# Layernorm variance by eight ScalarE squares with accumulators, and new issue lists

## The chip, the cores and the metric

The kernel runs on one core of a Trainium2 chip (trn2). The metric is the device time in microseconds of one execution. A core has five engines that run side by side, each with its own queue in order: TensorE (PE), VectorE (DVE), ScalarE (ACT), GpSimd (POOL) and SyncE (SP, which here only issues transfers).

## The reference, cut to what matters

A tower of four layers works on 32 sequences of 128 tokens with 64 features. Each layer is `h = h + attention(layernorm(h))` and then `h = h + ffn(layernorm(h))`:

```python
def _layernorm(x, axis=-1, eps=1e-05):
    m = jnp.mean(x, axis=axis, keepdims=True)
    v = jnp.var(x, axis=axis, keepdims=True)
    return (x - m) / jnp.sqrt(v + eps)
```

Layer 0 has attention with decay and a mixture of 16 experts, of which each token uses 2, and one more layernorm inside its ffn; layer 1 has block attention and 32 small experts, one for each token; layer 2 has linear attention with two inner layernorms and a mixture of 8 experts; layer 3 has a linear recurrence along the sequence and a layer with binary (sign) weights. That makes 11 layernorms over the 64 features of every token.

## The kernel before, in words

The 32 sequences are split into 4 units of 8. A unit's activations stand in SBUF as `h` and `xn`, 128 partitions (tokens of a sequence) by 8 sequences by 64 features, that is 128x512. Each unit has its own buffers, two PSUM banks and semaphores, and goes through the whole tower; the four units are independent, and the engines work on them in turn.

For each engine and unit the program is a Python generator (`program(u)`), which issues a few instructions between two `yield`s. Work that belongs to no unit (loading and preparing weights) stands in the generators `setup` and `later`. In which order an engine's queue takes the turns of these generators is written out by hand in `TURNS` (line 44): a string for each engine, where `s` is a turn of `setup`, `t` one of `later` and a digit one of that unit. `in_order` (line 85) plays it. An engine executes its queue strictly in that order, and each instruction waits for its semaphores.

A layernorm is done for a whole unit. DVE sums the features (line 1181) and subtracts the mean (line 1184, into `xn`). ACT squares `xn` with a scale of 1/8 (`square`, line 589, instruction at line 592) into `sq`. `sq` has 65 columns for each sequence: the last one holds epsilon, set once by POOL (line 449). So when DVE sums the 65 columns (line 1190, into `var`, 128x8), it gets variance plus epsilon. POOL raises that to the power -1/2 (`rstd`, line 471, instruction at line 474), DVE multiplies `xn` by it (line 1196, or 1207 for the norms whose result goes into `h`), and PE transposes the result (line 759). There are 11 norms in each of the 4 units, 44 in all. `sq` without its last column also serves as the buffer `y` (line 227), into which POOL gathers the embedding rows (line 441).

In the mixture of layer 0, PE multiplies by an expert's first weights (lines 764 and 765), DVE applies the ReLU as a floor and the gate (line 1286), and PE multiplies by the second weights (line 771). The gates reach all partitions by way of DRAM: SP saves them (line 408) and loads them spread (line 418). Ahead of that stand the routing steps on DVE (`top2`, 20 small steps for a unit). Unit 0's first gated product waits for the last of the prepared matrices of layer 3 (line 1276), unit 1's for the prepared sign weights (line 1279), because their raw data stand in the `hid` buffers of units 0 and 1. In layers 1 and 2, ACT evicts the hidden layer (line 620). In layer 3's last part, PE multiplies by the sign weights (line 1032), ACT evicts the result through Sign (line 711, 64 turns in each unit, 256 in all) and PE sums it up (line 1010). ACT's functions Exp, Gelu and Sin need tables of their own; each change of table is an instruction of its own in the trace (ACT_TABLE_LOAD).

Of the kernel before, what the change touches and what calls it, by code (L numbers as in the profile page):

```python
# [4 lines left out]
P = 128  # L5
D = 64
# [23 lines left out]
BIG = 1.0e30  # L30
LN_EPS = 1e-5
DEN_EPS = 1e-6
GATE_MIN = 2.0 ** -24
# [11 lines left out]
    "SP": (  # L45
        "st000001111100000000101010101010101010101012102222031012012033331202102101203313232121123313232121123332"
        "3222332323232323323232323233330000000010111111112222222323333233330123"
    ),
    "POOL": (
        "sttttttttt0ttttttt1ttttttttttt0tt21323000000111110123122223333203213000000111100211113222232333233223300"  # L50
        "0010110111222333223323"
    ),
    "ACT": (
        "sss00100211100031222011011ttt323322333232300000100110110011021020110302003020123011301322101002112321311"
        "30111233020222203212302312312300313232310231133323220300203130101301201022031133011001121312120223320032"
        "32301230230113203230002023101010103310101100110120100122310101332021021231031023023102123103102302310212"
        "31031230231021023131023023021023131023023120230132132032102130320132132012031032031231201203103203123120"
        "120310320312312012031032031231201231323123121231312323223323232233232322323333"
    ),
    "PE": (  # L60
        "st00001111tt00002221111001102003030030200302220010110103101300103311010011001011010210120130013101200122"
        "10210021212010011230203313233022101021011220303313233221211112230133032033122121032213233122032332233233"
        "32232133120132023013232233221320332320330310030113000002012010213213110321011031021102213111321020132310"
        "22222322322312312313033032033232332123131332320200033001301001010020202111331131011010101202121232320312"
        "30123023023230023001323002310030300100200001011201100011201103001011003112110311000210031101100113110000"
        "12001120110021130021132210022311002231102233110023311002233100223311002231102233110203311002233100223311"
        "00223110223311200331122331002233110022311002233101233110022133002233002231100223311023311002233002233112"
        "23001223300211330221133220033221130022113320013322001133022113322003112200331210033122003311220331122030"
        "11220033121003312200331122033112203011220033121003312200331122033112203011220033121003312203311223311223"
        "011223311233122331122331122311223312331223322332232233233223322332232233233223322332232332333333"  # L70
    ),
    "DVE": (
        "s000sss01t011t1ttt200122t0200ttt0113t03131001200000001000000103t11000111111010101111131t11111t1ttttttttt"
        "tt202t0t202202ttt02tt303202ttt30313031021232012222301302222130313330132320132303332210212323201333331030"
        "10120120120210210120331323021021012033103020302102010012030133203120122310032032001311210003210321311321"
        "30210320301201302300001112312312110001321311032122321321212211323312311113333123302000222032222322222000"
        "23330232333002002031311331230120322202131311333130130130311031010001022201210120100000010101100000012221"
        "32332232231212000001213331231111013313313323221132011001111112032323203020312303232132020321023120321230"
        "23123012302312032302310312031230231203203120333131030011230212101121123030311012312312332223021132332102"
        "32322210332233232133203232323123303223213330213021302130213023120321032103210321032130213213232323"  # L80
    ),
# [47 lines left out]
def tower(nc, ids, emb_w, logs, wa, wb, wc, wd, wup, wrow, binary, ballots, out):  # L129
# [6 lines left out]
    with ExitStack() as ctx:  # L136
# [68 lines left out]
        neg_half = sb("neg_half", [P, SEQS])  # L205
        floor0 = sb("floor0", [P, E0])

        h = per_unit("h", [P, SEQS, D])
        xn = per_unit("xn", [P, SEQS, D])
        sq = per_unit("sq", [P, SEQS, D + 1])  # L210
        total = per_unit("total", [P, SEQS])
# [14 lines left out]

        y = [sq[u][:, :, 0:D] for u in units]
        shifted = [view(fm2[u], 0, W, e=D) for u in units]
# [156 lines left out]
        with nc.Block() as block:  # L385
# [51 lines left out]
            def _(pool):  # L437
# [106 lines left out]
            def _(act):  # L544
# [498 lines left out]
            def _(dve):  # L1043
# [568 lines left out]
```

## Time and profile before

| | |
|---|---|
| three runs | 699.85, 701.21, 702.47 us (median 701.21) |
| the profiled execution, its own time | 703.61 us |
| its span, from the first to the last instruction | 701.8 us |
| mean granted TensorE clock | 0.886 of full speed |
| instructions | 8330 |

The profile is of one execution. Busy time is an engine's time with work on it; PEld is the loading of weights on TensorE, which overlaps the multiplications. In rows by line, `out<-in` are the program's names without the unit's number, then the shapes, the count, the busy time and the mean duration of one, then the engine's idle time before these instructions and what ended it. Two instructions of one engine can overlap, so that the busy time of a group is less than its count times the mean. The chain that ended last is followed back from the last instruction, step by step, to what released it.

### The profile page before, as it was taken

The page shows a single profiled execution, that of the slowest core. Times are in us where ns is not written, and L with a number is a line of the kernel's source. Part 1 is how long each engine was busy: PE and PEld are TensorE (multiplying, and loading weights), DVE is VectorE, ACT ScalarE, POOL GpSimd, SP SyncE. Part 2 cuts the span into 40 slices and gives each one's busy share as a digit, 9 for nine tenths or more (in the row PEclk, how much of TensorE's full clock was granted, in tenths as well). Part 3 has the DMA queues.
Part 4 walks back from the last instruction along what each step waited for, and adds up shares of the span by engine and source line. Part 5 has one row for each costly group of instructions (what it writes and reads, how often), then busy time and mean ns, then how long its engine had stood idle before and what let it go on. Part 6 is the DMA issues. An engine that isn't in the chain of part 4 may idle for free.

```text
span 701.8 us, 8330 instructions
## 1 busy us (share of the span) xinstructions
PE 582.4 (83%) x2951; PEld 319.9 (46%) x2974; DVE 491.8 (70%) x921; ACT 298.4 (43%) x525; POOL 185.6 (26%) x146
## 2 busy tenths in 40 slices
PE   0378669999999999899589677685897999999996
PEld 0166345444335445366454453345543644444442
DVE  0857779966678998967787988878888973333331
ACT  0222231100011122545356445342455379999985
POOL 6783001000031313420527235425216220000000
PEclk9965569999999999998699887765999999999999
DMA  8310234689564530000000013200420000000011
GB/s 212 105 20 1 60 126 134 211 224 337 189 186 154 160 125 32 1 1 2 0 1 0 1 31 124 75 15 6 162 78 1 1 0 1 1 0 1 0 31 30
DMA packets 30777, 49.85 MB, mean 71 GB/s; under 512 B 8400, under 2 KB 8656, under 8 KB 30736
## 3 DMA queue, kind: packets, MB, share of 16 engines
q1 hardware_dynamic: 29136, 46.82, 21.3%
q10 hardware_dynamic: 576, 1.45, 0.9%
q0 software_dynamic: 1024, 1.05, 0.7%
q8 instruction: 23, 0.38, 0.2%
q14 instruction: 18, 0.15, 0.1%
HBM read 47.86 MB, written 1.44 MB: 70 GB/s over the span
## 4 chain that ended last, share of the span: by engine, by line
PE 54%; DVE 26%; POOL 6%; issue 6%; DMA 4%; ACT 3%; SPq 1%; DVEq 0%; another core or an unknown queue 0%
PE ps L771 9%; PE ps L1032 9%; PE ps L1010 7%; PE ps L764 6%; POOL inv_std L474 4%; PE ps L765 4%; DVE hid L1286 2%; DVE total L1181 2%; PE ps L759 2%; POOL sq L441 2%; DVE xn L1196 2%; PE ps L1021 2%; DVE var L1190 2%; PE ps L886 2%; PE ps L823 2%
## 5 line engine op out<-in xcount | busy, mean ns | idle before, releaser
L711 ACT ACTIVATE hid<-ps 128x512 bf16<-128x512 f32 x256 | 134.0, 619 | 30.4 <-PE ps L1032 29.2
L474 POOL TENSOR_TENSOR inv_std<-var,neg_half 128x8 f32<-128x8 f32 x44 | 79.1, 1798 | 192.1 <-DVE var L1190 191.7
L1032 PE MATMUL ps<-xs,w3z 128*128 128x512 f32 x256 | 118.2, 535 | 5.5 <-DVE xs L1488 3.1
L764 PE MATMUL ps<-xs,up_hi 128*128 128x512 f32 x192 | 97.1, 506 | 21.2 <-DVE hid L1286 13.7
L1010 PE MATMUL ps<-hid,kbin 128*128 128x512 bf16 x248 | 96.2, 391 | 1.0 <-ACT hid L711 0.5
L1488 DVE TENSOR_TENSOR xs<-ps,big_a 128x512 fp32r<-128x512 f32 x64 | 43.5, 689 | 75.3 <-PE ps L1021 72.1
L765 PE MATMUL ps<-xs,up_lo 128*128 128x512 f32 x192 | 79.6, 415 | 0.0
L764 PEld LDWEIGHTS ps<-xs,up_hi 128*128 128x128 f32 x192 | 37.8, 197 | 91.3 <-issue 40.8
L771 PE MATMUL ps<-hid,kb 128*64 128x512 f32 x256 | 69.5, 633 | 0.0
L620 ACT ACTIVATE hid<-ps,kd 128x512 f32<-128x512 f32 x64 | 43.0, 685 | 59.3 <-PE ps L765 34.8
L1032 PEld LDWEIGHTS ps<-xs,w3z 128*128 128x128 f32 x256 | 49.8, 195 | 29.6 <-ACT hid L711 13.1
L1286 DVE SCALAR_TENSOR_TENSOR hid<-ps,floor,big_a 128x512 f32<-128x512 f32 x64 | 46.7, 744 | 14.4 <-PE ps L765 12.3
L592 ACT ACTIVATE sq<-xn 128x512 f32<-128x512 f32 x44 | 27.7, 629 | 67.4 <-DVE xn L1184 67.3
L759 PE MATMUL ps<-ka,xn 128*128 128x128 f32 x144 | 28.6, 333 | 26.3 <-DVE xn L1196 26.3
L1010 PEld LDWEIGHTS ps<-hid,kbin 128*128 128x128 bf16 x256 | 24.7, 97 | 50.0 <-issue 41.5
L771 PE MATMUL ps<-hid,kd 128*64 128x512 f32 x128 | 38.6, 693 | 5.4 <-DVE hid L1295 5.3
L765 PEld LDWEIGHTS ps<-xs,up_lo 128*128 128x128 f32 x192 | 38.5, 201 | 4.4 <-issue 1.9
L759 PEld LDWEIGHTS ps<-ka,xn 128*128 128x128 f32 x144 | 21.0, 173 | 36.8 <-DVE xn L1196 25.0
L1190 DVE TENSOR_REDUCE var<-sq 128x8 f32<-128x520 f32 x44 | 30.2, 686 | 8.1 <-ACT sq L592 7.7
L441 POOL DMA_INDIRECT sq<-emb_w,ids_sb x32 | 32.3, 1009 | 11.0 <-issue 9.2
L1196 DVE TENSOR_TENSOR xn<-xn,inv_std 128x512 f32<-128x512 f32 x36 | 28.1, 781 | 8.0 <-POOL inv_std L474 7.8
L603 ACT ACTIVATE xs<-ps 64x512 fp32r<-64x512 f32 x32 | 18.9, 591 | 33.3 <-PE ps L759 32.8
(252 smaller groups left out, 973.9 us busy)
## 6 DMA issues: line engine op xcount, KB each, us to landing
big_a<-gates_out SPq DMA_DIRECT2D x64, 256.0 KB, 3.9
fm<-gates_out SPq DMA_DIRECT2D x32, 256.0 KB, 3.9
xT<-gates_out SPq DMA_DIRECT2D x32, 256.0 KB, 3.9
big_a<-gates_out SPq DMA_DIRECT2D x32, 128.0 KB, 2.9
fm<-gates_out SPq DMA_DIRECT2D x16, 128.0 KB, 2.9
xT<-gates_out SPq DMA_DIRECT2D x16, 128.0 KB, 2.9
hid<-wup SPq DMA_DIRECT2D x4, 391.0 KB, 12.5
out<-h SPq DMA_DIRECT2D x4, 256.0 KB, 2.6
```

What stands on the lines that cost most here:

```text
L441: pool.indirect_dma_start(y[u][:, j, :], None, emb_w, bass.IndirectOffsetOnAxis(ap=ids_sb[:, SEQS * u + j:SEQS * u + j + 1].bitcast(U32), ...
L474: G.tensor_tensor(inv_std[u][:, :], var[u][:, :], neg_half[:, :], ALU.pow).then_inc(norm_rstd[u], 1)
L711: act.activation(sg[u][:, n % SUMS, :], b0, ACT.Sign).then_inc(s_made[u], 1)
L759: last = pe.transpose(b0[:, tile(t)], pair(xn[u], t), ident)
L764: pe.matmul(b0, up_hi[:, a:a + P], xs[u][:, l, :], start=True, stop=False)
L765: return pe.matmul(b0, up_lo[:, a:a + P], xs[u][:, l, :], start=False, stop=(name != "w1_1"))
L771: last = pe.matmul(ps[u][half(l), 1, :], weights, hid[u][:, l, m % RING, :], start=False, stop=stop)
L1010: pe.matmul(b1, chosen("sum3", n // BLOCKS % LANES, 0), sg[u][:, n % SUMS, :], start=(n == 0), stop=(n == LANES * GROUPS * BLOCKS - 1)).th ...
L1032: pe.matmul(b0, w3z[:, j, 2 * b:2 * (b + 1), :].rearrange("p i o -> p (i o)"), xs[u][:, l, :], start=True, stop=True).then_inc(w_made[u], 1)
L1190: V.tensor_reduce(var[u][:, :], sq[u][:, :, :], X, ALU.add).then_inc(norm_step[u], 1)
L1286: V.scalar_tensor_tensor(hid[u][:, l, e % RING, :], b0, floor0[:, e:e + 1], slots[u][i % SLOTS], ALU.max, ALU.mult).then_inc(hid_gated[u], 1)
L1488: V.tensor_tensor(xs[u][:, l, :], b0, big_a[u][:, l, :], ALU.mult).then_inc(u_made[u], 1)
```

## The change

The variance is computed by ACT alone. In place of one square of 128x512, ACT issues eight of 128x64, one for each sequence, each with an accumulator output that writes the sum over the 64 features into one column of `var`. Epsilon comes in as a bias: sqrt(epsilon / 64) is added to each scaled value before it is squared; the centred values sum to zero, so that the 64 squares sum to variance plus epsilon. The column for epsilon in `sq` goes, and with it DVE's sum and a step of the norm's count; POOL's power now waits for ACT. DVE's program is 11 turns shorter for each unit. All five lists of `TURNS` are new; their first units are now 0 and 2, then 1 and 3. Of the lists the diff below shows ACT's, and the beginning of DVE's.

```diff
--- before.py
+++ after.py
@@ -29,6 +29,7 @@
 ROWS = 32
 BIG = 1.0e30
 LN_EPS = 1e-5
+EPS_ROOT = (LN_EPS / 64.0) ** 0.5
 DEN_EPS = 1e-6
 GATE_MIN = 2.0 ** -24
 LOG2E = 1.4426950408889634
@@ -43,41 +44,41 @@
 TURNS = {
...
     "ACT": (
-        "sss00100211100031222011011ttt323322333232300000100110110011021020110302003020123011301322101002112321311"
-        "30111233020222203212302312312300313232310231133323220300203130101301201022031133011001121312120223320032"
-        "32301230230113203230002023101010103310101100110120100122310101332021021231031023023102123103102302310212"
-        "31031230231021023131023023021023131023023120230132132032102130320132132012031032031231201203103203123120"
-        "120310320312312012031032031231201231323123121231312323223323232233232322323333"
+        "sss0000020022200ttt2122113123133211333131300000000000202002002020002200210022131311302313102020232123202"
+        "11200323321212201311013030130210302021031203310323101312020333111323132232120113233220022102030102103120"
+        "23010131030101030013203103223010302012120230003322020200212020112300223321021010213203213201301201320321"
+        "32103102103203123102310120320132130213012032013213013210302132130132102301301321320123203103210312012302"
+        "313132121323213132121323213132121323213132121323213213113313131133131311313333"
     ),
...
     "DVE": (
-        "s000sss01t011t1ttt200122t0200ttt0113t03131001200000001000000103t11000111111010101111131t11111t1ttttttttt"
-        "tt202t0t202202ttt02tt303202ttt30313031021232012222301302222130313330132320132303332210212323201333331030"
...
+        "s000sss10tttt00tt2t02002tttt02tt00tttt00000000000000tt00000t0tttt220tt202t0tt0ttttt201103203120230220222"
+        "22021201202322210110222222013030113033201110230112110332031321313021310231310233102313130213102313302333"
...
@@ -204,10 +205,11 @@
         th = sb("th", [P, 8])
         neg_half = sb("neg_half", [P, SEQS])
         floor0 = sb("floor0", [P, E0])
+        eps_root = sb("eps_root", [P, 1])
 
         h = per_unit("h", [P, SEQS, D])
         xn = per_unit("xn", [P, SEQS, D])
-        sq = per_unit("sq", [P, SEQS, D + 1])
+        sq = per_unit("sq", [P, SEQS, D])
         total = per_unit("total", [P, SEQS])
         var = per_unit("var", [P, SEQS])
         inv_std = per_unit("inv_std", [P, SEQS])
@@ -224,7 +226,7 @@
         def view(ap, a, n, **sizes):
             return ap[:, a:a + n].rearrange("p (j e) -> p j e", **sizes)
 
-        y = [sq[u][:, :, 0:D] for u in units]
+        y = [sq[u][:, :, :] for u in units]
         shifted = [view(fm2[u], 0, W, e=D) for u in units]
         scaled = [v[u][:, :, 0:LANES * D].rearrange("p t (l d) -> p t l d", l=LANES) for u in units]
         lg, gk = ([view(fm[u], SEQS * E1 * i, SEQS * E1, e=E1) for u in units] for i in range(2))
@@ -322,7 +324,7 @@
         gate_in = [[sem(f"gate_in_{u}_{s}") for s in range(SLOTS)] for u in units]
 
         (LN_A0, LN_M0, LN_IN0, LN_A1, LN_M1, LN_A2, LN_IN2, LN_OUT2, LN_M2, LN_A3, LN_M3) = range(11)
-        NORM_SUM, NORM_CEN, NORM_VAR, NORM_OUT, NORM_N = 1, 2, 3, 4, 4
+        NORM_SUM, NORM_CEN, NORM_OUT, NORM_N = 1, 2, 3, 3
         (H_EMB, H_A0, H_M0, H_A1, H_M1, H_A2, H_M2, H_A3, H_OUT) = range(1, 10)
         (Y_IN0, Y_NUM2, Y_IN2, Y_OUT2) = range(1, 5)
         (X_A0, X_M0, X_A1, X_M1, X_A2, X_IN2, X_M2, X_A3, X_M3) = range(1, 10)
@@ -445,8 +447,7 @@
 
                 def setup():
                     yield
-                    for n in units:
-                        G.memset(sq[n][:, :, D:D + 1], LN_EPS)
+                    G.memset(eps_root[:, :], EPS_ROOT)
                     G.memset(neg_half[:, :], -0.5).then_inc(eps_set, 1)
                     pool.wait_ge(ids_in, 16)
                     for j in range(SEQS):
@@ -470,7 +471,7 @@
                 def program(u):
                     def rstd(ln):
                         yield
-                        pool.wait_ge(norm_step[u], norm_at(ln, NORM_VAR))
+                        pool.wait_ge(norm_sq[u], ln + 1)
                         G.tensor_tensor(inv_std[u][:, :], var[u][:, :], neg_half[:, :], ALU.pow).then_inc(norm_rstd[u], 1)
 
                     def shift(base, free, beta):
@@ -588,8 +589,13 @@
 
                     def square(ln):
                         yield
+                        if ln == LN_A0:
+                            act.wait_ge(eps_set, 1)
                         act.wait_ge(norm_step[u], norm_at(ln, NORM_CEN))
-                        act.activation(sq[u][:, :, 0:D], xn[u][:, :, :], ACT.Square, scale=float(D) ** -0.5).then_inc(norm_sq[u], 1)
+                        for j in range(SEQS):
+                            last = act.activation(sq[u][:, j, :], xn[u][:, j, :], ACT.Square, scale=float(D) ** -0.5,
+                                                  bias=eps_root[:, :], accum_out=var[u][:, j:j + 1])
+                        last.then_inc(norm_sq[u], 1)
 
                     def turned(use):
                         yield
@@ -1183,11 +1189,6 @@
                         dve.wait_ge(norm_step[u], norm_at(ln, NORM_SUM))
                         V.scalar_tensor_tensor(xn[u][:, :, :], spread(total[u][:, :], D), -1.0 / D, src[u][:, :, :],
                                                ALU.mult, ALU.add).then_inc(norm_step[u], 1)
-                        yield
-                        if u == 0 and ln == LN_A0:
-                            dve.wait_ge(eps_set, 1)
-                        dve.wait_ge(norm_sq[u], ln + 1)
-                        V.tensor_reduce(var[u][:, :], sq[u][:, :, :], X, ALU.add).then_inc(norm_step[u], 1)
 
                     def norm(ln, src, ready, value):
                         yield from centred(ln, src, ready, value)
```

## Rows read from the trace of the kernel before

**Rows 1.** The page: busy time, slices of DVE and ACT, chain by engine.

```profile
PE 582.4 (83%) x2951; PEld 319.9 (46%) x2974; DVE 491.8 (70%) x921; ACT 298.4 (43%) x525; POOL 185.6 (26%) x146
...
DVE  0857779966678998967787988878888973333331
...
ACT  0222231100011122545356445342455379999985
...
PE 54%; DVE 26%; POOL 6%; issue 6%; DMA 4%; ACT 3%; SPq 1%; DVEq 0%; another core or an unknown queue 0%
```

**Rows 2.** Windows: start:end, length, busy us (xinstructions) of PE, PEld, DVE, ACT, POOL, clock, DMA.

```profile
0.00:80.00 80.00, 41.93 (x168) 30.81 (x168) 44.75 (x115) 16.29 (x28) 46.30 (x56) 0.75 0.29 74
80.00:140.00 60.00, 49.62 (x206) 25.20 (x207) 54.05 (x146) 13.23 (x24) 3.44 (x2) 0.82 0.50 155
140.00:270.00 130.00, 124.39 (x763) 59.56 (x762) 99.75 (x160) 13.12 (x22) 19.11 (x14) 0.98 0.60 188
...
270.00:525.00 255.00, 204.02 (x1136) 122.07 (x1146) 209.94 (x390) 115.19 (x183) 96.65 (x62) 0.84 0.11 35
...
580.00:701.80 121.80, 115.24 (x476) 55.30 (x484) 36.96 (x54) 109.78 (x214) 0.00 (x0) 0.99 0.04 9
```

**Rows 3.** The chain by line, 270 to 400 and 400 to 525 us.

```profile
by line: POOL inv_std L474 13.9%; issue 7.1%; DVE xn L1196 5.9%; DVE var L1190 5.4%; DVE total L1181 5.3%; DVE xn L1184 3.9%; PE ps L886 3.3%; PE ps L918 3.1%; PE ps L771 3.0%; DVE xs L1218 2.7%; PE ps L920 2.6%; PE ps L759 2.4%; PE ps L764
...
by line: PE ps L771 10.7%; issue 8.8%; POOL inv_std L474 7.0%; DVE hid L1295 6.3%; PE ps L764 4.3%; PE ps L784 3.4%; SPq L418 3.1%; PE ps L765 3.0%; PE ps L759 2.9%; DVE var L1190 2.6%; DVE total L1181 2.5%; DMA fm<-gates_out 2.4%; DVE xn L
```

**Rows 4.** Timeline, three hand-overs, square to power: start, duration, line.

```profile
273.99 0.63 ACT L592 ACTIVATE sq<-xn 128x512 f32<-128x512 f32 x1
...
275.67 0.67 DVE L1190 TENSOR_REDUCE var<-sq 128x8 f32<-128x520 f32 x1
...
276.42 1.65 POOL L474 TENSOR_TENSOR inv_std<-var,neg_half 128x8 f32<-128x8 f32 x1 [2.22 <-DVE var L1190]
...
303.22 0.63 ACT L592 ACTIVATE sq<-xn 128x512 f32<-128x512 f32 x1 [0.88 <-DVE xn L1184]
...
303.88 0.70 DVE L1190 TENSOR_REDUCE var<-sq 128x8 f32<-128x520 f32 x1 [0.70 <-ACT sq L592]
...
304.66 1.64 POOL L474 TENSOR_TENSOR inv_std<-var,neg_half 128x8 f32<-128x8 f32 x1 [3.65 <-DVE var L1190]
...
493.92 0.62 ACT L592 ACTIVATE sq<-xn 128x512 f32<-128x512 f32 x1
...
497.98 2.03 POOL L474 TENSOR_TENSOR inv_std<-var,neg_half 128x8 f32<-128x8 f32 x1 [9.56 <-DVE var L1190]
```

**Rows 5.** Groups by line, ACT and DVE: busy us, mean ns | idle before.

```profile
L711 ACT ACTIVATE hid<-ps 128x512 bf16<-128x512 f32 x256 | 134.0, 619 | 30.4 <-PE ps L1032 29.2
L620 ACT ACTIVATE hid<-ps,kd 128x512 f32<-128x512 f32 x64 | 43.0, 685 | 59.3 <-PE ps L765 34.8 <-remote 13.1 <-PE ps L905 11.0
L592 ACT ACTIVATE sq<-xn 128x512 f32<-128x512 f32 x44 | 27.7, 629 | 67.4 <-DVE xn L1184 67.3
...
L597 ACT ACTIVATE xT<-ps 128x512 f32<-128x512 f32 x16 | 9.5, 596 | 33.6 <-PE ps L759 33.6
...
L608 ACT ACT_TABLE_LOAD x3 | 3.8, 1283 | 0.1
...
L608 ACT ACTIVATE gs<-gs 128x8 f32<-128x8 f32 x8 | 1.7, 207 | 20.6 <-DVE gs L1260 20.6
...
L1190 DVE TENSOR_REDUCE var<-sq 128x8 f32<-128x520 f32 x44 | 30.2, 686 | 8.1 <-ACT sq L592 7.7
```

**Rows 6.** Timeline of ACT, two 128x1 copies in a row.

```profile
94.15 0.16 ACT L582 ACTIVATE bqk<-ps 128x1 f32<-128x1 f32 x1
94.20 0.17 ACT L583 ACTIVATE bqk<-ps 128x1 f32<-128x1 f32 x1
```

**Rows 7.** Timeline of DVE, the first gated product of unit 0.

```profile
92.83 0.74 DVE L1286 SCALAR_TENSOR_TENSOR hid<-ps,floor,big_a 128x512 f32<-128x512 f32 x1
```

**Rows 8.** The waits, longest first: us in total, times, longest.

```profile
POOL inv_std L474 <- DVE var L1190: 191.7, 32, 33.8
```

More of the change, by code:

```diff
@@ L45 @@
     "SP": (
-        "st000001111100000000101010101010101010101012102222031012012033331202102101203313232121123313232121123332"
-        "3222332323232323323232323233330000000010111111112222222323333233330123"
+        "st000000000000000000000202222002002020202020202022212111123212123333112121232331231231231321321312312312"
+        "3131313131313131313131313133330000000002222222221111131133331133330213"
     ),
     "POOL": (
-        "sttttttttt0ttttttt1ttttttttttt0tt21323000000111110123122223333203213000000111100211113222232333233223300"
@@ L51 @@
-        "0010110111222333223323"
+        "stttttttt0ttttttttttttttt02tttttt21313000000022222210231113133130000300100322222221220030111130333110331"
+        "0133222222111313313313"
     ),
     "ACT": (
-        "sss00100211100031222011011ttt323322333232300000100110110011021020110302003020123011301322101002112321311"
-        "30111233020222203212302312312300313232310231133323220300203130101301201022031133011001121312120223320032"
-        "32301230230113203230002023101010103310101100110120100122310101332021021231031023023102123103102302310212"
@@ L59 @@
+        "32103102103203123102310120320132130213012032013213013210302132130132102301301321320123203103210312012302"
+        "313132121323213132121323213132121323213132121323213213113313131133131311313333"
     ),
     "PE": (
-        "st00001111tt00002221111001102003030030200302220010110103101300103311010011001011010210120130013101200122"
-        "10210021212010011230203313233022101021011220303313233221211112230133032033122121032213233122032332233233"
-        "32232133120132023013232233221320332320330310030113000002012010213213110321011031021102213111321020132310"
@@ L64 @@
[L64 to L68, printed above, removed]
@@ L69 @@
-        "11220033121003312200331122033112203011220033121003312200331122033112203011220033121003312203311223311223"
-        "011223311233122331122331122311223312331223322332232233233223322332232233233223322332232332333333"
+        "st0000tt022000200200000000020121002021000001030030230200130010112000223002033322020022020022020022021002"
+        "13022032212112121121221231032320310233012312132313212130123131223123130122310203131223123131023102310310"
+        "31031031330123010120312031031203131031231313103310130233303032211112330320102322222232122011202033312121"
@@ new lines @@
+        "32111201302310130310031020021032013031330303131210123123033311103303220221112232223302022002002001001000"
+        "31200300110021003120310010013002003102001330031003320013020032003200122002202210022100003002122032200212"
+        "32200003200220322001220012200210022302213211200223110021130022113322010332201133220011332001132200113322"
+        "10033221103322110033211003221100331220033110223311002233112003112200133220011330221133002211332001132200"
+        "13322001133022113300113322113002133002211332211330011330221130022133002113300113322113322003112203312200"
@@ L71 @@
+        "33211003322110033112230112233102233113321133221132211332213322113321133221132211332213322113321133221132"
+        "211332213322113321133221132211332213321133211331131133133113311331131133133113311331131331333333"
     ),
     "DVE": (
-        "s000sss01t011t1ttt200122t0200ttt0113t03131001200000001000000103t11000111111010101111131t11111t1ttttttttt"
-        "tt202t0t202202ttt02tt303202ttt30313031021232012222301302222130313330132320132303332210212323201333331030"
-        "10120120120210210120331323021021012033103020302102010012030133203120122310032032001311210003210321311321"
@@ L76 @@
[L76 to L80, printed above, removed]
+        "s000sss10tttt00tt2t02002tttt02tt00tttt00000000000000tt00000t0tttt220tt202t0tt0ttttt201103203120230220222"
@@ new lines @@
+        "22021201202322210110222222013030113033201110230112110332031321313021310231310233102313130213102313302333"
+        "30220100212100102012123023312031023012300132013200130012000312312031200312000003120312031031222312312223"
+        "13213123123122231222310200231220312321311300301012131330020210230323131022221311021131311101003331003033"
+        "31033013130111102322313010310230130303030300000000000222302222202200200002221011222201003233011123120011"
+        "21121333123222222331332332202201013120220202020313131100032313311211111132112330121333313213001230132333"
@@ L81 @@
+        "31111313123223333032121212021231232131220232221332301113222133101311113210331113333132131303133312130133"
+        "231023102310231023103210312301231023123123123123131313"
     ),
```

## The prediction

> **What bounds the kernel now.** I read the page first: TensorE (PE) is busy for 83% of the span, VectorE (DVE) 70%, ScalarE (ACT) 43%, and in the slices the ACT row is low until about slice 16 while the DVE row is high nearly everywhere [rows 1]. An average hides stages, so next came the windows [rows 2]. Four stages show. Up to 80 us the weights are prepared. From 80 to 140 DVE is busy for 54.1 of 60 us: it is the bound there. From 140 to 270 PE has 124.4 of 130 us (the first expert loop). From 270 to 525 no engine is full (PE 204, DVE 210, ACT 115 of 255 us). From 580 on ACT has 109.8 and PE 115.2 of 121.8 us: the Sign evictions.
>
> The norms that the change touches lie mostly in the stage from 270 to 525, so I read the chain that ended last there [rows 3]. What the reader is to see: the POOL power (line 474) has 13.9% of the first half and 7.0% of the second, and the DVE variance sum (line 1190) 5.4% and 2.6%. At about 0.6 us for each, 5.4% of 130 us and 2.6% of 125 us are 7.0 and 3.3 us; counted piece by piece it is 16 passes. Each pass goes sum, then power, then the multiplication. The chain enters a norm mostly through DVE's own queue and hardly ever through the ACT square.
>
> So the unit of the change is the hand-over: from the start of the square to the start of the power. The shortest is the norm at 303.22 us: square 0.63, sum 0.70, power at 304.66, together 1.44 us [rows 4]. The first of the sixteen takes 2.43 us (273.99 to 276.42) because its sum waits behind other DVE work until 275.67; the last takes 4.06 us (493.92 to 497.98) [rows 4]. Over the sixteen, taken by start times, the median is 2.2 us. What is beyond 1.44 us is queueing, mostly for DVE, and after the change nothing of a norm's variance waits for DVE.
>
> **The change, part by part.**
>
> *Eight squares for one.* ACT issues 44 x 8 instructions of 128x64 in place of 44 of 128x512. Their price, B for a block of eight, is not in the trace; I build it. From 128x8 to 128x512 (SBUF to SBUF) a duration rises from 207 to 629 ns [rows 5], 0.837 ns a column, so 64 columns are 254 ns. A bias read from a tile adds 685 - 596 = 89 ns (line 620 against 597): 343 ns. Two in a row overlap: line 711 lasts 619 ns, but 134.0 us / 256 is 523 ns, so 96 ns [rows 5]. Start to start 247 ns, and B = 8 x 0.247 + 0.096 = 2.07 us if the accumulator costs nothing. That is the lower end.
>
> *The accumulator's output.* No row shows one. Its nearest row is a 128x1 ACTIVATE, 0.16 and 0.17 us long, of which two follow each other after 0.05 us [rows 6]. Upper end: each sum is written by such a step, and nothing overlaps: 8 x (0.343 + 0.165) = 4.1 us. I take the step with the usual overlap of 96 ns, since every pair of neighbours in the rows overlaps: 0.069 us each, 8 x 0.316 + 0.096, B = 2.6 us. The Trainium skill ("VectorE: DVE Perf Modes", Two Vector instructions with no wait between them) says that on VectorE an operation with an accumulator output is two instructions, the second one reading the accumulator; it says so of VectorE alone, and no run here shows it for ACT. If it held for ACT too, it would speak for the upper half.
>
> *The hand-over after.* B + 0.08 us (in the shortest one the power starts 0.78 us after a sum of 0.70 us) = 2.69 us, against 2.2 us: +0.5 us x 16 passes = +8 us. With the ends of B: 2.15 us, so 0, and 4.14 us, so +31 us.
>
> *ACT's load.* 44 x (2.6 - 0.63) = +87 us: 298 becomes 385 us (55%). Between 270 and 525, 27 squares add 53 us to 115, which is 66% of the stage. What queues behind a block are evictions, line 620 above all (685 ns each), and PE waits for them. I cost this at nothing, since ACT still has a third of the stage free; without that cover each eviction caught would pay up to 2 us. Behind 580 us there is no square. The Trainium skill ("Perfetto Trace Analysis", Optimizing Scalar/DVE Operations) has both sides: if VectorE is saturated, moving work to ScalarE may make sense, and grouping into larger operations helps an engine that is saturated. The rows put the first condition nearer than the second.
>
> *The sum leaves DVE.* Line 1190 is 44 x 686 ns = 30.2 us of busy time [rows 5]. Sixteen are in the hand-overs already. The other 28, at 0.6 us each, free 17 us of DVE; DVE has 26% of the whole chain [rows 1] but more of it in the dense stages, so I take a third, -6 us (bounds 0 and -17).
>
> *One memset for four, a tile of 512 columns for 520, the wait for the epsilon moved to ACT.* POOL has a few small memsets less ahead of gathers that wait for the ids, and epsilon is set ahead of those gathers, whose result the first square needs anyhow: nothing, either way. The memset of epsilon hides behind the gathers; without that cover, the first square and what ACT has behind it would be later by that memset.
>
> *The new lists.* Three things can be counted in them. (a) Units run in the order 0, 2, 1, 3. Unit 0's first gated product (line 1286) has 107 DVE turns ahead of it in the old list and 67 in the new, because the routing of other units comes later; the turns of the preparation ahead of it are 24 in both. It starts at 92.83 us now [rows 7]. A DVE instruction up to 80 us takes 44.75 / 115 = 0.39 us, so PE's expert loop could start 40 x 0.39 = 16 us earlier. The moved turns come due in a stretch where DVE is 90% busy, so I take half, -8 us (bounds 0 and -16). (b) When the last unit's last square is issued, 33 Sign evictions are out in the old ACT list and 42 in the new: 9 x 0.523 = -5 us from the ACT-bound tail (bounds 0 and -5). (c) ACT changes between the Exp, Gelu and Sin tables 12 times instead of 10; a load is 1.283 us [rows 5]: 2.6 us of ACT, +1 us on the path (bounds 0 and +3). The SP and POOL lists keep the number of their turns; the gate loads follow the units, and I cost that at nothing because PE has 96% of the stage that they feed.
>
> *Sum.* +8 + 1 - 6 - 8 - 5 = -10 us. The profiled execution took 703.61 us (span 701.80, 1.8 us around it), 2.4 us above the median of the three runs, 701.21. On the median: 691 us.
>
> **The rivals.**
>
> *1. The blocks are long (slower, 714 us).* The mechanism: each of the eight sums is read out by a step that doesn't overlap, in the block between line 1184 and line 474. For it: the sum must be complete before it can be written, and the power stands on the path with 13.9%. Against it: all neighbours in the ACT rows overlap. Price: +31 + 1 - 6 - 8 - 5 = +13 us. The gains of the other parts are 19 us less 1; 16 passes eat 18 us at a hand-over of 3.3 us, so this decides from B = 3.2 us on.
>
> *2. DVE was the whole limit (676 us).* For it: DVE is the bound from 80 to 140 and the densest engine with 82% from 270 to 525, and POOL waits 191.7 us in all for the sum [rows 8]. B stays near 2.1 us (0), DVE's relief comes two thirds through (-11), the start comes three quarters through (-12), tail -5, tables +1: -27 us, which on the median gives 674; I take 676, since not all of it will be on the path. Against it: a wait of POOL is mostly a lack of work, and DVE's freed slots are scattered.
>
> *3. The order gives nothing at the front (about 700 us).* The PE loop starts earlier, runs alone on unit 0 and waits for DVE as before; then only +8 + 1 - 6 - 5 = -2 us is left. For it: DVE does the same work up to 140 us, less the sums. A part of it would be a change of the lists that doesn't do what it says.
>
> **How the numbers follow.** Chances: forecast 0.38, rival 1 0.33, rival 2 0.15, rival 3 0.14. The forecast's own range is 683 to 699 us. All bounds together would give 663 and 735 us; the range that leaves out 2 in 10 is 672 to 720 us, from rival 2 with 4 us to spare to rival 1 with some evictions caught behind blocks. About 0.5% (3.5 us) is what a measurement can tell from no change. Faster: most of the forecast and rival 2, 0.49. Same: the rest of the forecast and most of rival 3, 0.16. Slower: rival 1 and a remainder, 0.35. Cases of both signs hold much of the chance, so the likeliest one's range stands above.
>
> **What the changed profile would show.** The block: start to start of the 128x64 squares 0.25 to 0.31 us, ACT busy near 385 us; over 0.4 us means rival 1. The hand-over near 2.7 us with no long ones, POOL's wait now put down to ACT. DVE busy near 462 us. Line 1286 first starting between 77 and 88 us. Twelve table loads. PE busier from 80 to 140 us. The forecast is wrong if B is over 3.2 us, if line 620 waits in numbers behind squares, or if the expert loop ends no earlier than now.

## The result and the profile after

The changed kernel is slower: the median is 719.25 us (715.10 to 720.75, 4 runs) against 700.53 us for the kernel before on the same chip, and the ratio is 1.031 with a 95% interval of 1.027 to 1.036. The forecast was 691 us, faster. The value lies inside the stated range of 672 to 720 us, next to the 714 us of rival 1, but on the other side from the forecast. Here and below, single executions that took 1.5% or more above the fastest of the same kernel are left out of the ratios, though not of the medians: 3 of 10 in the run with the new lists and the old arithmetic, at 709 to 710 us, and 3 of the 13 executions of the kernel before beside it.

From the page of the kernel after (busy time and the chain by engine), to be read against [rows 1]:

```profile
span 716.9 us, 8972 instructions
PE 583.0 (81%) x2974; PEld 320.3 (45%) x2974; DVE 460.0 (64%) x877; ACT 391.3 (55%) x1187; POOL 180.8 (25%) x143
...
PE 52%; DVE 17%; ACT 15%; POOL 7%; issue 6%; DMA 2%; SPq 0%; DVEq 0%; POOLq 0%
```

ACT went from 298 to 391 us, DVE from 492 to 460 us. In the chain DVE fell from 26% to 17% and ACT rose from 3% to 15%: the path moved from DVE's queue to ACT. In the stage from 270 to 525 us (columns as in [rows 2]):

```profile
270.00:525.00 255.00, 196.01 (x1075) 116.95 (x1073) 181.57 (x350) 160.49 (x555) 91.53 (x60) 0.81 0.11 34
```

ACT now has 160 of 255 us (63%), and DVE and PE each did less than before in the same time; the granted clock of PE is 0.81 of full speed where it was 0.84. The groups of ACT at the line of the squares (columns as in [rows 5]):

```profile
L596 ACT ACTIVATE sq<-xn,eps_root 128x64 f32<-128x64 f32 x352 | 117.1, 335 | 68.1 <-DVE xn L1190 68.0
L596 ACT ACTIVATION_READ_ACCUMULATOR sq<-xn,eps_root 128x1 f32 x352 | 66.4, 189 | 0.0
```

The accumulator output is an instruction of its own on ACT, 189 ns long, one behind each square. Here is a hand-over, the first one, on the timeline of ACT and POOL:

```profile
22.73 0.33 ACT L596 ACTIVATE sq<-xn,eps_root 128x64 f32<-128x64 f32 x1
22.97 0.18 ACT L596 ACTIVATION_READ_ACCUMULATOR sq<-xn,eps_root 128x1 f32 x1
23.06 0.33 ACT L596 ACTIVATE sq<-xn,eps_root 128x64 f32<-128x64 f32 x1
...
25.29 0.18 ACT L596 ACTIVATION_READ_ACCUMULATOR sq<-xn,eps_root 128x1 f32 x1
...
25.56 1.89 POOL L475 TENSOR_TENSOR inv_std<-var,neg_half 128x8 f32<-128x8 f32 x1 [2.43 <-ACT sq L596]
```

Square to square it is 0.33 us: 0.24 us to the readout and 0.09 us from there to the next square. The block lasts until 25.47 us, 2.74 us, and the power starts 2.83 us after the first square, where the shortest old hand-over took 1.44 us [rows 4]. Blocks further on last 2.77 us.

What else the block does can be seen on the timeline of ACT and PE around 405 us. Two units have the hidden layer of an expert ready in PSUM, one at 405.45 us and the other with the product of line 911 at 406.15 us. Both evictions stand behind the block of a third unit, which began at 404.47 us:

```profile
404.47 0.34 ACT L596 ACTIVATE sq<-xn,eps_root 128x64 f32<-128x64 f32 x1
...
405.76 0.39 PE L911 MATMUL ps<-xT,kbin 128*128 128x512 bf16 x1
...
407.13 1.24 ACT L626 ACTIVATE hid<-ps,kd 128x512 f32<-128x512 f32 x2
408.42 0.19 PEld L770 LDWEIGHTS ps<-xs,up_hi 128*128 128x128 f32 x1 [2.07 <-ACT hid L626]
```

The weight load of line 770 waits for 2.07 us, 0.9 us of it while the squares of the third unit run and the rest while the two evictions, held up by them, follow each other. The chain that ended last goes through this place (start, duration), from the squares to an eviction and not to a power:

```profile
406.37 0.85 ACT sq L596 x5
407.22 1.15 ACT hid L626 x2
```

The whole chain has 28 stretches of squares, 78 us together. Followed piece by piece, 16 of them (45 us) run into the power of a norm, and behind the other 12 (33 us) stands other work of ACT, evictions above all.

### The profile page after: what moved, and what is told of

The parts are those of the page before. It is cut to its first block, busy times and chain, and to the rows that moved or that the text cites. A ratio compares the mean times of both kernels' runs of the same rounds, so it can differ in the third digit from the quotient of the medians.

```text
span 716.9 us, 8972 instructions
## 1 busy us (share of the span) xinstructions
PE 583.0 (81%) x2974; PEld 320.3 (45%) x2974; DVE 460.0 (64%) x877; ACT 391.3 (55%) x1187; POOL 180.8 (25%) x143
## 3 DMA queue, kind: packets, MB, share of 16 engines
HBM read 47.86 MB, written 1.44 MB: 69 GB/s over the span
## 4 chain that ended last, share of the span: by engine, by line
PE 52%; DVE 17%; ACT 15%; POOL 7%; issue 6%; DMA 2%; SPq 0%; DVEq 0%; POOLq 0%
ACT sq L596 11%; PE ps L1038 9%; PE ps L777 9%; PE ps L1016 7%; PE ps L770 5%; POOL inv_std L475 5%; PE ps L771 4%; DMA hid<-wup 2%; PE ps L765 2%; POOL sq L443 2%; PE ps L892 2%; PE ps L1027 2%; DVE hid L1287 2%; DVE xn L1190 2%; DVE xn L1197 1%
## 5 line engine op out<-in xcount | busy, mean ns | idle before, releaser
L596 ACT ACTIVATE sq<-xn,eps_root 128x64 f32<-128x64 f32 x352 | 117.1, 335 | 68.1 <-DVE xn L1190 68.0
L717 ACT ACTIVATE hid<-ps 128x512 bf16<-128x512 f32 x256 | 134.9, 623 | 31.0 <-PE ps L1038 29.1
L475 POOL TENSOR_TENSOR inv_std<-var,neg_half 128x8 f32<-128x8 f32 x44 | 75.5, 1716 | 251.7 <-ACT sq L596 251.7
L1016 PE MATMUL ps<-hid,kbin 128*128 128x512 bf16 x256 | 100.7, 395 | 0.6 <-ACT hid L717 0.5
L596 ACT ACTIVATION_READ_ACCUMULATOR sq<-xn,eps_root 128x1 f32 x352 | 66.4, 189 | 0.0
```

Source lines behind the costliest of these rows:

```text
L596: last = act.activation(sq[u][:, j, :], xn[u][:, j, :], ACT.Square, scale=float(D) ** -0.5, bias=eps_root[:, :], accum_out=var[u][:, j:j + 1])
L717: act.activation(sg[u][:, n % SUMS, :], b0, ACT.Sign).then_inc(s_made[u], 1)
L1016: pe.matmul(b1, chosen("sum3", n // BLOCKS % LANES, 0), sg[u][:, n % SUMS, :], start=(n == 0), stop=(n == LANES * GROUPS * BLOCKS - 1)).th ...
```

## The experiments

The kernel before ran beside each experiment on the same chip; its medians lie between 697.7 and 699.2 us, and the ratios below are to them. Two theories went in first. P: the block lengthens the path through each norm. L: the new lists are the loss.

**Old lists, new arithmetic.** The changed kernel with the lists of before, less the 44 DVE turns of the sum.

The other four lists are the old ones; of DVE's the first line stands here.

```diff
     "DVE": (
-        "s000sss10tttt00tt2t02002tttt02tt00tttt00000000000000tt00000t0tttt220tt202t0tt0ttttt201103203120230220222"
+        "s000sss1t011tttt200122t000ttt113t031310012000000000000010t11000111111010101111131t11111t1ttttttttttt202t"
...
```

> The new arithmetic (eight squares with accumulators) under the old lists, of which only the 44 DVE turns of the variance sum are taken out. Theory P (the block of 2.77 us sits on the path in place of a hand-over of 1.44 us): slower than before by 10 to 40 us, 711 to 740 us. Theory L (the new lists are the loss, the arithmetic is neutral): 696 to 705 us.

Measured: 737.7 us, ratio 1.055 (1.050 to 1.060), +38 us, as theory P had it.

**New lists, old arithmetic.** The kernel before with the new lists; the turn of the sum is put two turns behind the subtraction of the mean.

The other four lists are the new ones.

```diff
     "DVE": (
-        "s000sss01t011t1ttt200122t0200ttt0113t03131001200000001000000103t11000111111010101111131t11111t1ttttttttt"
+        "s000ss0s10tttt00tt2t02002t02ttt02tt00tttt00000000000000tt00000t0tttt220tt202t0tt0ttttt201210312031202302"
...
```

> The old arithmetic (one square of 128x512, the DVE sum over 65 columns) under the new lists, with the DVE turn of the sum put two turns behind the one that subtracts the mean. Theory P: the new lists alone gain, 685 to 697 us. Theory L: the lists are the loss, 710 us or more.

Measured: 698.2 us, ratio 0.999 (0.995 to 1.004). So theory L falls: the new lists alone cost nothing, and the loss comes with the new arithmetic. They gain nothing either, which theory P had expected them to. With the eight squares they are worth 5.5% - 3.1% = 2.4%, some 16 us: the same lists are worth more with the long blocks than without; why was not tried. The windows of this run show what became of the earlier start:

```profile
0.00:80.00 80.00, 33.97 (x132) 23.15 (x134) 45.66 (x141) 17.36 (x30) 42.12 (x53) 0.73 0.39 92
80.00:140.00 60.00, 54.71 (x252) 28.20 (x252) 51.13 (x105) 12.26 (x20) 8.98 (x5) 0.90 0.46 141
```

Line 1286 starts at 75.0 us in place of 92.8, but PE has 34.0 us of work up to 80 us where it had 41.9, and 54.7 against 49.6 us up to 140 [rows 2]: together 2.9 us less. The routing and attention work of the other units, which the old order did first, is put off, and the last gated product of the loop starts at 283.9 us in place of 279.8.

**One square for eight.** To see what the length of the block is worth; the variance is left out.

```diff
-                        for j in range(SEQS):
-                            last = act.activation(sq[u][:, j, :], xn[u][:, j, :], ACT.Square, scale=float(D) ** -0.5,
-                                                  bias=eps_root[:, :], accum_out=var[u][:, j:j + 1])
-                        last.then_inc(norm_sq[u], 1)
+                        act.activation(sq[u][:, 0, :], xn[u][:, 0, :], ACT.Square, scale=float(D) ** -0.5,
+                                       bias=eps_root[:, :], accum_out=spare[u][:, 0:1]).then_inc(norm_sq[u], 1)
```

> The changed kernel with one square of 128x64 and one readout for each norm in place of eight; the power reads a constant, so the variance of all sequences is left out. The block falls from 2.77 to about 0.43 us, and 44 x 2.33 = 103 us of ACT go. Theory P with the chain's count (the block has 11% of the chain, 28 passes): 719 - 28 x 2.3 = 655 us. With the 16 passes of the prediction: 682 us. Theory L: hardly less than 719.

Measured: 672.5 us, ratio 0.963 (0.957 to 0.969), 47 us below the changed kernel.

**Twelve squares for eight.** The four that are added take 0.306 us each with their readouts, and the block lasts 3.98 us.

```diff
+                        for j in range(4):
+                            last = act.activation(sink[u][:, j, :], idle[:, :], ACT.Square, scale=float(D) ** -0.5,
+                                                  bias=eps_root[:, :], accum_out=spare[u][:, j:j + 1])
                         last.then_inc(norm_sq[u], 1)
```

> The changed kernel with four more squares (128x32, bf16 out, with readout) behind the eight of each norm and ahead of its signal: the block grows by some 1.2 us to 4.0 us. Theory P: +28 x 1.2 = +34 us (753 us) by the chain's count, +19 us (738 us) by 16 passes. Theory L: 719 to 725 us.

Measured: 775.3 us, ratio 1.111 (1.104 to 1.117), +56 us. That is more than either count of passes gave: 46 us for each us of a block, more than one for every one of the 44 norms.

A part of this may be the clock. From 270 to 525 us PE is busy for 184 us in this run, 196 us in the changed kernel and 202 us under the new lists with the old arithmetic; its granted clock there is 0.75, 0.81 and 0.85 of full speed, and over the whole span the same 2974 instructions keep PE busy for 603.6, 583.0 and 572.2 us. In these runs a PE that waits more goes with a lower clock and slower products, 11 and 21 us from one run to the next. How much of that lies on the path was not tried.

**No readouts.** The variance is left out here too: the power reads a constant.

```diff
...
-                                                  bias=eps_root[:, :], accum_out=var[u][:, j:j + 1])
+                                                  bias=eps_root[:, :])
```

> The changed kernel with the eight squares but no accumulator output; the power reads a constant, so the variance is left out. The block is 8 x 0.239 + 0.1 = 2.0 us in place of 2.77 (0.093 us less for each readout). If each us of a block costs what lies between the one-square run and the changed kernel (47 us for 2.33 us, 20 us for one): 703 us. If it costs as steeply as above 2.77 us (46 us for one): 684 us.

Measured: 694.1 us, ratio 0.994 (0.989 to 0.998). The block is 2.00 us on the timeline:

```profile
22.95 2.00 ACT L598 ACTIVATE sq<-xn,eps_root 128x64 f32<-128x64 f32 x8
```

The four points under the new lists, as block length and ratio: 0.43 us 0.963; 2.00 us 0.994; 2.77 us 1.031; 3.98 us 1.111. At 699 us for 1, a us of a block costs 13, 34 and 46 us from one point to the next. It grows steeper. The eight readouts, 0.77 us of each block, cost 3.8%: 26 us. Without them the changed kernel would be slightly faster than before, were its sums not missing.

A block has two effects, though: it lengthens the hand-over, and it occupies ACT. Two runs split them.

**Occupation without length.**

```diff
                         act.activation(sq[u][:, 0, :], xn[u][:, 0, :], ACT.Square, scale=float(D) ** -0.5,
                                        bias=eps_root[:, :], accum_out=spare[u][:, 0:1]).then_inc(norm_sq[u], 1)
...
+                        for j in range(SEQS):
+                            last = act.activation(sink[u][:, j, :], idle[:, :], ACT.Square, scale=float(D) ** -0.5,
+                                                  bias=eps_root[:, :], accum_out=spare[u][:, j + 1:j + 2])
+                        last.then_inc(norm_sq[u], 1)
```

> As the one-square run (672 us), but ACT then does eight more squares (128x32, with readout, on a constant tile) behind the norm's signal: the hand-over stays 0.5 us, and ACT is as busy as in the changed kernel. The variance is left out. Theory H (the hand-over's length is the loss): 672 to 682 us. Theory O (ACT's occupation is the loss, since evictions wait behind blocks): 705 to 720 us.

Measured: 702.3 us, ratio 1.006 (1.003 to 1.009). Against 0.963 that is 4.3%, 30 us, for squares whose results nothing reads. Neither theory by itself gives that: H had 672 to 682, O at least 705.

**Length without occupation.**

```diff
+                        G.tensor_tensor(twice[u][:, :], var[u][:, :], neg_half[:, :], ALU.pow).then_inc(norm_rstd[u], 1)
                         G.tensor_tensor(inv_std[u][:, :], var[u][:, :], neg_half[:, :], ALU.pow).then_inc(norm_rstd[u], 1)
...
```

The multiplication waits for the second power.

> As the one-square run (672 us), but POOL takes the power twice, the first time into a spare tile: the hand-over to the multiplication grows by 1.65 us and ACT does no more work; POOL goes from 27% to 38% busy. The variance is left out. Theory H: +1.65 x 20 = 33 us, 700 to 710 us. Theory O: 672 to 680 us.

Measured: 715.5 us, ratio 1.024 (1.018 to 1.031). That is 6.1%, 43 us for 1.65 us a norm: 26 us for each us. POOL's other work is held up too, so that this is an upper price of length. A longer step does draw more norms onto the path here: powers stand in 23 places of the chain, against 6 in the one-square kernel. The two effects, measured each by itself from the one-square kernel, add up to more than both together in the changed kernel (47 us). I take it that they use the same slack; that is not shown.

**Occupation under the old lists.** The same question asked of the kernel before.

```diff
                         act.activation(sq[u][:, :, 0:D], xn[u][:, :, :], ACT.Square, scale=float(D) ** -0.5).then_inc(norm_sq[u], 1)
...
+                        for j in range(SEQS - 1):
+                            last = act.activation(sink[u][:, j, :], idle[:, :], ACT.Square, scale=float(D) ** -0.5,
+                                                  bias=eps_root[:, :], accum_out=spare[u][:, j:j + 1])
+                        last.then_inc(norm_sq[u], 1)
```

> The kernel before, arithmetic and lists untouched, but ACT does seven small squares on a constant tile (128x32, bf16 out, with readout, 0.306 us each, 2.1 us in all) behind the signal of each norm's square. ACT is then as busy as with the eight squares under the old lists (0.63 + 2.1 = 2.8 us for a norm), while every hand-over has its old length. That change cost 38 us (699 to 737 us). Theory O (ACT's occupation): as under the new lists, where 44 x 2.45 us behind the signal cost 30 us, 26 us: 720 to 730 us. Theory H (the hand-over's length): 699 to 706 us.

Measured: 724.5 us, ratio 1.035 (1.028 to 1.042), +25 us. It has every DVE sum of before, and from the start of a square to the power a norm takes no longer (median 1.95 us, before 1.98). But a square can now stand behind another unit's squares: from the subtraction to the square the median is 0.49 us in place of 0.03. That delay belongs to ACT's occupation, and from the subtraction to the power it adds up to 6.5 us over all 44 norms. So of the 38 us that the eight squares cost under the old lists, ACT's occupation alone reproduces about two thirds, and some 13 us are left for the longer hand-overs less what DVE gains. The waits say where (the kernel before, then this run, then the one with old lists and eight squares: who waited for which eviction, us in total, times, longest):

```profile
PEld ps L764 <- ACT hid L620: 14.5, 15, 2.8
```

```profile
PEld ps L780 <- ACT hid L636: 29.9, 22, 4.9
```

```profile
PEld ps L770 <- ACT hid L626: 29.1, 20, 4.9
```

The lines are the same operation in each: PE's next expert product, and the eviction in front of it. Its weight load waited 14.5 us for evictions before, 29.9 us with squares that nobody waits for and 29.1 us with the eight squares; the longest wait went from 2.8 to 4.9 us. The two experiments agree nearly number for number. Under the new lists the same wait doubles as well (the old arithmetic, then the changed kernel):

```profile
PEld ps L764 <- ACT hid L620: 9.4, 12, 1.9
```

```profile
PEld ps L770 <- ACT hid L626: 18.4, 12, 3.3
```

The catches can be counted. These are the weight loads of PE that waited for an eviction, of whatever line, while squares ran on ACT between the moment the eviction's input was ready and its start, and the time of those squares:

| run | caught | us of squares |
|---|---|---|
| kernel before | 1 | 0.5 |
| seven squares behind each signal, old lists | 16 | 21.5 |
| eight squares, old lists | 16 | 21.7 |
| old arithmetic, new lists | 1 | 0.4 |
| changed kernel | 11 | 13.6 |

For the run with squares that nobody waits for, the 21.5 us are most of its 25 us. And most of the loss arises in one place: unit 0's tenth norm comes 83.1 us after its ninth in the kernel before and 100.0 us after it in this run. Between the two stands layer 2's mixture, with its evictions at line 620 (636 in this run).

**The first four norms alone.** Eight squares for the norms of layer 0 and the first of layer 1.

```diff
+                        if ln in BY_ACT:
...
+                            for j in range(SEQS):
+                                last = act.activation(sq[u][:, j, 0:D], xn[u][:, j, :], ACT.Square, scale=float(D) ** -0.5,
+                                                      bias=eps_root[:, :], accum_out=var[u][:, j:j + 1])
+                        else:
+                            last = act.activation(sq[u][:, :, 0:D], xn[u][:, :, :], ACT.Square, scale=float(D) ** -0.5)
+                        last.then_inc(norm_sq[u], 1)
```

> Eight squares for the first four norms of each unit alone (the two of layer 0, its inner one and the first of layer 1: 16 of the 44), the old arithmetic for the other 28, under the new lists with the sum two turns behind. The new arithmetic cost 21 us under these lists (698 to 719 us). If the loss is even over the norms: 698 + 16/44 x 21 = 706 us. If it arises where ACT is busy and no engine bounds, from 270 us on: 696 to 700 us.

Measured: 708.2 us, ratio 1.016 (1.011 to 1.021). That is 11 us above the old arithmetic under the new lists, half the loss, from 16 of the 44 norms; the even share was 8 us. But the traces don't put the loss where most of these norms are. Four of the 16 squares stand behind 270 us, and at about 300 us this run is 3 to 5 us behind the run with the old arithmetic. When the last square of all starts, which both take in the old way, it is 11.3 us behind (576.6 against 565.3 us). In the changed kernel it is the same: unit 0's sixth square starts at 268.4 us against 267.7 us, 0.7 us behind, and the last square of all at 585.0 us, 19.7 us behind. So nearly all of the loss arises behind 270 us, where ACT is busiest before the tail. What costs the run with 16 norms its last 6 to 8 us, after its new arithmetic is over, stays open: DVE's list is another one too, and the next runs differ by as much under lists that are nearly the same.

**Where the sum stands in DVE's queue.** Three placements under the new lists with the old arithmetic: two turns behind the subtraction is above (0.999).

Here is the first line of DVE's list with two turns and then, as three edits, with one, with one to three by the durations of what lies between, and with three:

```diff
-        "s000ss0s10tttt00tt2t02002t02ttt02tt00tttt00000000000000tt00000t0tttt220tt202t0tt0ttttt201210312031202302"
+        "s000s0ss10tttt00tt2t0200202tttt02tt00tttt00000000000000tt00000t0tttt220tt202t0tt0ttttt202110132031202303"
+        "s000ss0s10tttt00tt2t02002t02ttt02tt00tttt00000000000000tt00000t0tttt220tt202t0tt0ttttt202110132031202303"
+        "s000sss010tttt00tt2t02002tt02tt02tt00tttt00000000000000tt00000t0tttt220tt202t0tt0ttttt201120321031202302"
```

> The old arithmetic under the new lists as in the run before of that kind (698 us, as before), with the DVE turn of the variance sum one turn behind the subtraction in place of two. The square takes 0.63 us, about one DVE instruction, so DVE should now wait for it in places: if DVE's queue is what a norm waits for, 698 to 705 us; if the hand-over's length counts alone, 690 to 697 us.

Measured: 709.1 us, ratio 1.016 (1.011 to 1.020).

> The old arithmetic under the new lists, with each variance sum placed as many DVE turns behind its subtraction as cover about 0.65 us, the square's length (1 to 3 turns). Theory H with queues in order (a sum that comes too early stalls the whole DVE queue, one that comes late lengthens the hand-over): below both fixed placements (698 us for two turns, 709 us for one): 688 to 697 us. If the placement hardly matters and 698 and 709 us are scatter of the order: 698 to 709 us.

Measured: 701.7 us, ratio 1.006 (1.001 to 1.010).

> The same with three turns for nearly all norms. No DVE wait for a square is left, but the hand-over is longer by one DVE instruction of up to 0.7 us: if stalls of DVE are what counts, 690 to 698 us; if the hand-over's length counts, at 20 us for one us, 705 to 712 us.

Measured: 712.4 us, ratio 1.023 (1.016 to 1.031). The waits of the runs with one, two and three turns, in this order:

```profile
DVE xn L1196 <- POOL inv_std L474: 10.6, 12, 1.7
...
DVE var L1190 <- ACT sq L592: 8.4, 15, 0.9
```

```profile
DVE xn L1196 <- POOL inv_std L474: 16.0, 15, 1.8
...
DVE var L1190 <- ACT sq L592: 0.9, 3, 0.4
```

```profile
DVE xn L1196 <- POOL inv_std L474: 24.6, 22, 1.8
```

One turn too early, and DVE, with all that is queued on it, stands still 15 times for a square; one turn later, and it waits longer for the power. Against two turns these runs are 1.6 and 2.4% slower by their ratios, half to three quarters of what the new arithmetic costs under these lists. Two things speak against reading much into it. The waits above add up to 19.0, 16.9 and 24.6 us, which is 2 and 8 us more than with two turns, where 11 and 17 us were lost. And the kernel with two turns itself took 696 to 710 us from one execution to the next, so that the 709 us lie within its spread. The timed placement, meant to be best, is no better than the fixed one; its 701.7 us is what was expected if the placement hardly matters. So runs with other lists differ by 1 to 2%; what makes that difference is not shown. Of the versions that compute the variance none beat the kernel before; the new lists with the old arithmetic tie with it.

## Why the prediction was wrong

*The block.* B was right: 2.6 us forecast, 2.77 us measured. Taking the nearest row for the readout, a 128x1 ACTIVATE with the usual overlap, was sound; the readout lasts 189 ns and not 165, and its step is 0.093 us and not 0.069. What the Trainium skill says of VectorE ("VectorE: DVE Perf Modes", Two Vector instructions with no wait between them), that an accumulator output is a second instruction, the trace shows for ACT: 352 of them, one for each square.

*The step that failed is ACT's load*: "I cost this at nothing, since ACT still has a third of the stage free". The load itself was forecast well (385 us, measured 391; 66% of the stage, measured 63%). But evictions on PE's path don't use an average: each one caught waits for the rest of a block that stands ahead of it in ACT's queue, four times as long as the old square. Measured by itself it is +25 us under the old lists and 30 us above the one-square kernel under the new. I had written down the price of an eviction caught, up to 2 us; what I didn't do is count how many could be caught. In the changed kernel 11 were, for 13.6 us, and in its chain 12 blocks with 33 us stand in front of other work of ACT. Two of the signs that the prediction had named for being wrong came: line 620 waits behind squares, and the expert loop ends later than before (its last gated product starts at 286.4 us, before at 279.8).

*The hand-over.* +8 us was forecast for 16 passes. The count of passes did not rise: in the chain after, the squares have 11% of 717 us, 28 blocks, but only 16 of these run into a power, 8 of them from 270 to 525 us, where the forecast had counted its 16. My expectations for the experiments took all 28 for norms on the path; 12 of them are the occupation of the last paragraph. The price of length is 26 us for each us (an upper price), not 16; with both effects together a us of a block costs 13, 34 and 46 us, and a part of that may be PE's clock. Under the old lists 13 us are left after the occupation, where my sum for hand-over and DVE's relief was +8 - 6 = +2 us; so this term was too small as well, but by less than half of what the occupation was. How the 13 us divide is open.

Of the two sides that the Trainium skill gives ("Perfetto Trace Analysis", Optimizing Scalar/DVE Operations), moving work off a busy VectorE and keeping operations large, the first was the nearer by its condition, and the runs went against it: the relief of DVE, at 82% of the stage, did not outweigh eight small pieces for one on ACT. The second is said of a saturated engine, and ACT was at 45% (63% after); the pieces cost all the same, by what stood behind them.

*DVE's relief*, -6 us, could not be seen by itself; if it is there, it is in the 13 us. DVE is busy 32 us less, and its share of the chain fell from 26% to 17%, while ACT's rose by 12 points.

*The lists.* -12 us forecast (front, tail, tables). With the old arithmetic they are worth nothing (0.999), with the new 16 us. That the second number is near the forecast is luck, since of the forecast's reasons the front failed and the tail gave 2 us. The front part failed as rival 3 said: the loop starts 18.9 us earlier (73.9 us) and ends later, since what was taken out from in front of it is due within it. The tail part held in direction, at half its size: from the last square to the end of the span it is 132.6 us before and, with the new lists and the old arithmetic, 130.2 us. The trace has the 12 table loads that were counted in the list; what they cost on the path was not tried.

*The rivals.* Rival 1 came nearest in time and had the wrong point: slower from B = 3.2 us on, while 2.77 us was enough, because occupation was missing from its sum. Rival 2 (676 us, with B near 2.1 us and no sum on DVE) is answered by the run without readouts, which has just that, a block of 2.00 us and no sum: 694 us. Rival 3 was right on the front and wrong as a whole.

## What to carry to other kernels

When work moves to an engine that is half idle, don't ask whether it has room in the stage; ask what else is in its queue, who waits for that, and how long the longest uninterrupted piece is that it can now stand behind. A count of passes on the old chain prices the steps that wait for the new work; the work that stands behind it in the queue has to be counted apart. And an accumulator output on small tiles is paid for by a second instruction each: eight here were 0.77 us of a 2.77 us block, which decided between 0.994 and 1.031 of the time before.

## What was not expected of the hardware

A square of 128x64 with a bias read from a tile lasts 333 ns and can be followed after 0.24 us; the readout lasts 187 ns (median) and is followed after 0.09 us, so that both overlap with their neighbours. And lists that do the same work in nearly the same order differ: with the 44 DVE turns of the sum moved by one place the time was 11 and 17 us longer by the ratios, as much as several of the larger terms of the prediction, though the spread between executions of one list (696 to 710 us) is of that size too.
